# Other orders of TensorE's and ScalarE's steps, and the rank table one head earlier, in a sandwich layer with top-64 attention

## The reference

```
q, k, v: 16 heads of 64;  16 memory keys and values go in front
dots = einsum('bhid,bhjd->bhij', q, k) * scale
dots = einsum('bhij,hk->bkij', dots, pre_proj)      # heads mixed
dots = where(causal, neg, dots)
vk   = top_k(dots, 64)[0][..., -1:]                 # 64th largest of each row
attn = softmax(where(dots < vk, neg, dots))
attn = einsum('bhij,hk->bkij', attn, post_proj)     # heads mixed again
out  = einsum('bhij,bhjd->bhid', attn, v) @ Wo + bo
```

## Time and profile before

| | |
|---|---|
| median of 3 runs | 4002.94 us (3998.09 to 4003.88) |
| the profiled execution | 4003.49 us |
| its span | 4001.7 us |
| granted TensorE clock, mean | 0.846 |
| busy, of the span: TensorE | 2863.9 us (72%) |
| VectorE | 2996.8 us (75%) |
| ScalarE | 2842.3 us (71%) |
| GpSimd | 1982.1 us (50%) |
| loads and stores of SyncE's queue | 16.03 MB, 1.4% of the transfer engines |

### The profile page before, as it was taken

One profiled execution on the slowest core, in us unless ns is written; L12 is line 12 of the kernel. 1 busy time (PEld: TensorE's weight loads), 2 busy tenths in 40 slices (PEclk: granted clock), 3 DMA queues, 4 the chain that ended last, 5 costly groups with the idle time before them and its releaser, 6 DMA issues. The chain is left out here.

```text
span 4001.7 us, 71286 instructions
## 1 busy us (share of the span) xinstructions
PE 2863.9 (72%) x13751; PEld 2023.4 (51%) x13751; DVE 2996.8 (75%) x14030; ACT 2842.3 (71%) x7482; POOL 1982.1 (50%) x3688
## 2 busy tenths in 40 slices
PE   7777777777767777677777767777677777777664
PEld 4445545555545555545555544555455555455543
DVE  3787777777777777777777777777777777777774
ACT  1777777777757777777777757777677777777772
POOL 3345545545444555545545444554545555454543
PEclk9888888888878888888888878888888888888876
DMA  1000000000000000000000000000000000000000
GB/s 37 6 2 2 4 7 4 8 4 7 2 4 7 4 7 2 5 7 4 7 4 7 2 4 7 4 7 2 4 7 4 7 2 5 7 4 7 2 7 3
DMA packets 31417, 22.76 MB, mean 6 GB/s; under 512 B 3201, under 2 KB 30338, under 8 KB 30722
## 3 DMA queue, kind: packets, MB, share of 16 engines
q1 hardware_dynamic: 30722, 16.03, 1.4%
HBM read 11.83 MB, written 4.19 MB: 4 GB/s over the span
## 5 line engine op out<-in xcount | busy, mean ns | idle before, releaser
L882 ACT ACTIVATE signs<-scores,state 128x528 int8<-128x528 f32 (+2 forms) x2304 | 1445.7, 628 | 369.6 <-DVE state L1113 308.4
L1300 POOL TENSOR_SCALAR probs<-probs,rinv 128x528 f32<-128x528 f32 (+3 forms) x1024 | 538.9, 545 | 1838.3 <-DVE rinv L1142 1836.6
L737 PE MATMUL y_bank<-u_all,probsT 128*128 128x128 f32 x5120 | 997.8, 378 | 2.1 <-ACT probsT L893 2.1
L737 PEld LDWEIGHTS y_bank<-u_all,probsT 128*128 128x128 f32 x5120 | 936.4, 284 | 23.3 <-issue 11.6
L1308 POOL TENSOR_TENSOR work<-scores,work 128x528 f32<-128x528 f32 (+3 forms) x1024 | 887.0, 898 | 13.8 <-DVE work L1027 13.8
L726 PE MATMUL s_bank<-xn,gT 128*128 128x512 f32 (+3 forms) x2048 | 698.4, 463 | 6.2 <-ACT gT L814 3.6
L765 PE MATMUL misc<-missed,onesP 128*1 128x5 f32 x512 | 49.6, 168 | 908.8 <-ACT u_all L814 460.2
L1137 DVE SCALAR_TENSOR_TENSOR probs<-scores,kth,expo 128x528 f32<-128x528 f32 (+3 forms) x1024 | 521.4, 565 | 114.7 <-issue 68.0
L765 PEld LDWEIGHTS misc<-missed,onesP 128*1 128x1 f32 x512 | 22.4, 81 | 1117.6 <-ACT u_all L814 507.2
L1027 DVE TENSOR_SCALAR_CACHE_REDUCE work<-scores,state 128x528 f32<-128x528 f32 (+3 forms) x1024 | 527.6, 553 | 43.3 <-DVE state L1113 43.3
L903 ACT ACTIVATE expo<-scores,negmax 128x528 f32<-128x528 f32 (+3 forms) x1024 | 537.6, 580 | 0.0
(11 more groups left out here) (152 smaller groups left out, 3590.6 us busy)
## 6 DMA issues: line engine op xcount, KB each, us to landing
xwork<-in_L_attn_x_dram SPq DMA_DIRECT2D x17, 256.0 KB, 2.8
xres<-in_L_attn_x_dram SPq DMA_DIRECT2D x16, 256.0 KB, 3.2
out_dram<-ybuf SPq DMA_DIRECT2D x16, 256.0 KB, 2.4
u_all<-in_L_attn_Wq_dram SPq DMA_DIRECT2D x1, 512.0 KB, 3.7
u_all<-in_L_attn_Wk_dram SPq DMA_DIRECT2D x1, 512.0 KB, 4.4
u_all<-in_L_attn_Wv_dram SPq DMA_DIRECT2D x1, 512.0 KB, 5.4
u_all<-in_L_attn_Wo_dram SPq DMA_DIRECT2D x1, 512.0 KB
expo<-in_L_ffn_w_gate_dram SPq DMA_DIRECT2D x1, 192.0 KB, 4.9
```

What stands on the lines that cost most here:

```text
L737: mm = nc.tensor.matmul(y_bank[:, t * P:(t + 1) * P], lhsT=probsT[:, h % 2, at:at + P], rhs=u_all[:, j, h * D:(h + 1) * D], start=False, s ...
L882: nc.scalar.activation(signs[:, k, 0:ROW[t]], row(scores, ring(head_of(s, k + 1), RING), t), ACT.Sign, bias=guesses(s % STATES, k, GUESSES ...
L1300: nc.gpsimd.tensor_scalar(prb, prb, rinv[:, slot_p, t:t + 1], 1.0, ALU.mult, ALU.mult).then_inc(scaled, 1)
```

## The change

Four streams are reordered; no instruction is added or taken away but the wait that is moved.

1. TensorE: in a step, weigh and the turns 0 and 1 now come directly after the product for the next head, then FLAG, then turn 2, and E1 last. The memory part of y (`memory_y`) moves from the end of step 6 to step 7, ahead of weigh.
2. ScalarE: T0 now stands between E0 and the copy of G, T1 between FLAG and count(0), T2 after E1, and all four exponentials stand last.
3. VectorE: the wait for the exponentials moves from in front of the branch on missed rows to directly in front of `probs`.
4. GpSimd: the rank table is made one step earlier, for the head of age 5, at the same place in GpSimd's step.

```
 TensorE
                     make_extra(kind, b, par, s, 0)
                     if makes_g(kind, s):
                         product_g(kind, b, par, par if s < H - 1 else 1 - par, s + 1)
+                    if s == LAG_V and kind != "first":
+                        memory_y(kind, b)
+                        if kind != "drain":
+                            pe.wait_ge(y_taken, b)
+                            start_y()
+                    if lagged(kind, s, LAG_V):
+                        weigh(head_of(s, LAG_V), g - LAG_V)
+                    if lagged(kind, s, LAG_P):
+                        turn(head_of(s, LAG_P), g - LAG_P, 0)
+                        turn(head_of(s, LAG_P), g - LAG_P, 1)
                     if flagged(kind, s):
                         pe.wait_ge(bad_ready, g - LAG_E + 1)
                         share(kind, b, ("FLAG", s))
                         nc.tensor.matmul(misc[...][0:1, 0:T + 1], lhsT=onesP[:, 0:1], ...)
-                    if s == LAG_V and kind in ("mid", "last"):
-                        pe.wait_ge(y_taken, b)
-                        start_y()
-                    if lagged(kind, s, LAG_V):
-                        weigh(head_of(s, LAG_V), g - LAG_V)
+                    if lagged(kind, s, LAG_P):
+                        turn(head_of(s, LAG_P), g - LAG_P, 2)
                     make_extra(kind, b, par, s, 1)
-                    if lagged(kind, s, LAG_P):
-                        for q in range(3):
-                            turn(head_of(s, LAG_P), g - LAG_P, q)
-                    if s == LAG_V - 1 and kind != "first":
-                        memory_y(kind, b)
 ScalarE
                     take_extra(0)
+                    take_turned(0)
                     if makes_g(kind, s):
                         take(kind, b, par, ("G", s + 1), gT[(s + 1) % 2][:, :])
                     if flagged(kind, s):
                         at_least(act, probs_ready, 4 * (g - LAG_E))
                         take(kind, b, par, ("FLAG", s), flags[:, :], ...)
+                    take_turned(1)
                     count(0)
                     take_extra(1)
-                    take_turned(0)
-                    exponentials(0)
-                    exponentials(1)
-                    take_turned(1)
-                    exponentials(2)
-                    exponentials(3)
                     take_turned(2)
+                    for p in range(T):
+                        exponentials(p)
 VectorE
                     if applies:
-                        dve.wait_ge(exp_ready, 4 * gp + 4)
                         at_least(dve, t_full, 3 * (gp - 1))
...
                                     general_kth(slot_p, t)
+                        dve.wait_ge(exp_ready, 4 * gp + 4)
+                        alone(dve)
                         for t in ORDER:
                             v.scalar_tensor_tensor(out=probs[...], ...)
 GpSimd
-                    if lagged(kind, s, LAG_P):
-                        at_least(pool, kth_ready, g - LAG_P)
-                        pool.wait_ge(found_ready, 4 * (g - LAG_P) + 4)
+                    if lagged(kind, s, LAG_E):
+                        at_least(pool, kth_ready, g - LAG_E)
+                        pool.wait_ge(found_ready, 4 * (g - LAG_E) + 4)
                         alone(pool)
                         nc.gpsimd.tensor_tensor(offset[:, :, 0:9], ranks,
-                                                found[:, s % 2, :].unsqueeze(2).to_broadcast([P, T, 9]),
+                                                found[:, (s - 1) % 2, :].unsqueeze(2).to_broadcast([P, T, 9]),
                                                 ALU.add).then_inc(offset_ready, 1)
```

## The result

The changed kernel takes 3628.4 us, median of four runs (3623.95 to 3633.7), against 4002.9 us before: the ratio is 0.9068, interval [0.905, 0.9086]. (A fourth execution of the kernel before took 5645.7 us, for a reason that isn't known, and isn't counted.) The gain is 375 us. The forecast was 3545, the range 3485 to 3730: the time lies inside, 83 us above the forecast. The profiled execution took 3627.61 us, its span is 3625.8.

What follows compares the result with a forecast made beforehand. The prediction took a circle of waits between VectorE and GpSimd as the bound. Step times summed to 206.4 us a batch against 236.6; the gain, taken as 458 from 4003.5, gave 3545 us, range 3485 to 3730.

Steps and rivals of the forecast that it cites:

- The wait of 513.7 us: VectorE's pick of the 64th value (L1044) waiting 240 times for GpSimd's rank table; claimed to go entirely.
- plain steps: Steps without extra work (1, 3 to 6, 13, 14), bound by VectorE at 12.0 us, plus 0.15 for a longer gap.
- the steps with GpSimd's product: Steps 10 to 12, counted from moves to moves: VectorE's moves wait for GpSimd's product, 13.1 us each before the added 0.15.
- Rival B: TensorE's clock falls in its idle time ahead of turn 0, delaying ScalarE: 3745 us, half of it 3650; chance 0.20.
- the slack that the forecast gave ScalarE: ScalarE's counts finish 1.3 us before the moves need them, its exponentials 1.5 us before probs need them.
- D: GpSimd's rank table still too late, or another equally long wait takes its place: 3950 to 4003 us; chance 0.02.
- C: TensorE stays at 1.2 GHz and sets the step, delaying ScalarE's counts: 4750 us; chance 0.03.
- the rule that speaks against it: VectorE's two-SBUF-input instructions and GpSimd's SBUF reads fully block each other at the shared port; some 17 us per batch.
- rival A: Port blocking between VectorE and GpSimd: about 3 us in four steps, 0.3 to 0.5 elsewhere; 3800 us, chance 0.11.
- the late norm of x: In step 2, TensorE's first product waits for the norm of step 1, making turn 0 late: 13.6 us for the step.
- 453 and 8: The gain over 15 batches at 30.2 us each, and 8 or so from the first batch and the end.
- three steps of 13.1: Steps 10 to 12, where the moves wait for GpSimd's product, entered in the batch sum as 39.4 us.

Runs made afterwards that it cites:

- e4: The changed kernel with TensorE's FLAG product put back ahead of weigh and the turns, ScalarE's new order kept: 4395.21 us.
- e11: The changed kernel with GpSimd's norm products and residual sums in the loop cut to 8 of 128 columns a tile, the norm of x left whole: 3548.27 us.
- e7: The changed kernel with GpSimd's norm products and residual sums in the loop cut to 8 of 128 columns a tile, for x too: 3594.66 us.
- e5: The changed kernel with one more GpSimd product (two SBUF inputs, 128x512, result unused) behind the rank table in each step: 3866.52 us.
- e8: The changed kernel with each norm's two GpSimd products over 512 columns replaced by four one-pass instructions over 128 columns each: 3574.41 us.
- e9: The changed kernel with the norms' two 512-column products in the loop moved from GpSimd to ScalarE, GpSimd making only the 4-column factors: 3558.2 us.
- one half of this change: The changed kernel with the rank table back in GpSimd's own step, so the new orders of the other engines alone: 3940.78 us.
- e12: The changed kernel with one more GpSimd instruction (one SBUF input, 640 columns, constants, result unused) behind the rank table in each step: 3729.23 us.
- e6: The changed kernel with one more GpSimd instruction, a memset of 975 columns, behind the rank table in each step: 3623.6 us.

## Why the prediction came out as it did

What the change takes away was foreseen rightly, and the rest in part. The wait of 513.7 us went; plain steps take 12.0 to 12.3 (12.0 to 12.3 forecast); ScalarE's times in the step shown are met within 0.2 us but for the exponentials, 0.7 earlier; the steps with GpSimd's product take 13.25 to 13.27 (13.25), though by the block and not by the wait. Rival B's idle time of TensorE ahead of turn 0 is there (708.8 us), and ScalarE waits for T0 for 203 us in all, but the slack that the forecast gave ScalarE takes it. D is refuted by the missing wait, C by the granted clock of 0.90; e4 shows that C's ring is real, with FLAG as its weakest link.

The step that failed is the rule that speaks against it, which became rival A and got 0.11. The port is blocked; the forecast put its price at nothing, and the price is the 80 us that e11 gives back. Rival A, taken whole, was wrong too, in size: it gave 17 us per batch, 3 in four steps and 0.3 to 0.5 in the rest. Measured by the steps of e7 the four steps (0, 2, 8 and 9) cost 2.0, 1.4, 2.1 and 0.8, 6.4 in all, and the rest next to nothing: beside GpSimd's small instructions L1044 takes 0.24 to 0.30 us in a plain step, in the mean, for 0.22.

The reading that led there was the earlier trace rows: L979 started 0.26 before GpSimd's product ended, and took 2.40 for 2.29, "0.11 is there at most" where a full wait would show 0.26. The rows of e5 show what a full wait looks like: an instruction of 0.17 us, blocked, ends about 0.01 behind its blocker (up to 0.04 in the rows after the change), so about 0.14 of its own time has run by then. For L979 that makes 61.85 + 2.29 - 0.14 = 64.00, and it ended at 63.99. The 2.29 was another instruction's time, but it holds for L979 itself: in e8, where GpSimd has the one-pass norm beside it, which lets such instructions through, L979 takes

```profile
60.36 2.29 DVE L979 SCALAR_TENSOR_TENSOR probs<-a_all 128x2048 f32<-128x2048 f32 x1 [3.79 <-ACT a_all L809]
```

The row that was taken to refute the block is just what a block looks like. Step 2 was right by luck: I had given the late norm of x 1.6 us by way of TensorE, and it cost 1.3 by the block of L1105 and L1110. In e9, where both take their 0.18 and 0.17 us again, the step falls by 1.2.

Two sums in the forecast are off by little: 453 and 8 make 461, and 458 was taken; three steps of 13.1 make 39.3, and 39.4 was taken.

## What to carry to other kernels

Where a wait is removed between VectorE and GpSimd, they come to work side by side; look then which of VectorE's instructions have two SBUF inputs, and give GpSimd's SBUF reads of that stretch to an engine with idle time, as e9 does. Look for the block in busy times, not in waits: a small instruction that ends with the other engine's. When a row seems to refute a rule by a tenth of a microsecond, work out what the rule would have shown in that row, start-up included, before the chance is set. And orders of two engines that wait for each other are to be changed together: one half of this change is worth 62 us alone, and the whole of it but FLAG's move is 392 us slower than the kernel before.

## What the runs showed of the hardware

- VectorE's instructions with two SBUF inputs are held up to the end of a GpSimd instruction over 512 or 640 columns that reads SBUF, with one input or two, and not by a memset of 0.91 us (e5, e12, e6). One that comes 0.07 us behind the start of such an instruction gets through: L1108 took its usual 0.11 beside L1224, 14 times in the changed kernel.
- How long GpSimd's instruction takes doesn't tell how long it blocks. Beside its power over four columns (L1217, 1773.87 to 1774.91) L1044 took its usual 0.23 us, and the four instructions of e8 (0.8 us for 128 columns with two per-row scalars) let VectorE's two-input instructions through at their usual times, or 0.15 to 0.21 later. That it goes by the columns read fits the rows, and wasn't tried by itself. The Trainium skill (SBUF — State Buffer, section on the two separate sides) says that the pair is held for the whole instruction; these rows don't agree, as far as GpSimd's times in the profile can be trusted, which are rough.
- The block goes both ways: beside probs GpSimd's copy of 8 columns took 0.61 us for 0.19 (e8).
- On GpSimd, (x - a) * b with two per-row scalars took 0.8 us over 128 columns, where constants over 640 columns took 0.73; cutting two passes to one made the norm longer, 3.16 for 2.1.
